# Scale and offset of the first feed-forward norm moved from GpSimd to VectorE

## The reference

```
x1  = x + attention(x, context)
h   = ln(ln(x1, g2, be2), gf, bf)          # two norms, one after the other
x2  = x1 + gelu(h @ w1 + b1) @ w2 + b2
ln(x, g, b) = (x - mean) * rsqrt(var + eps) * g + b
```

## Time and profile before

| | us |
|---|---|
| median of 3 runs | 493.59 (488.44 to 493.99) |
| the profiled execution | 494.68 |
| its span, first to last instruction | 492.4 |
| VectorE busy | 316.4 (64%) |
| GpSimd busy | 123.6 (25%) |
| granted TensorE clock, mean | 0.919 |

### The profile page before, as it was taken

How to read it: one execution, slowest core, us unless ns; L and a number is a source line. 1 busy time by engine, 2 the same in 40 slices (tenths; PEclk the granted TensorE clock), 3 DMA queues, 4 the chain that set the end, 5 groups by cost and what they waited for, 6 DMA issues and landing times.

```text
span 492.4 us, 20265 instructions
## 1 busy us (share of the span) xinstructions
PE 395.4 (80%) x8885; PEld 277.8 (56%) x8885; DVE 316.4 (64%) x909; ACT 262.9 (53%) x451; POOL 123.6 (25%) x113
## 2 busy tenths in 40 slices
PE   3667687998879978997899888988897888397765
PEld 1335554665557655765576647655676566255553
DVE  5433777769537894888578847787568666615331
ACT  2556455565355656564746554765565657154331
POOL 7001017024303070216021511134012401612000
PEclk9965999999789999999999989998999999879575
DMA  7766008324702382236422442236022012102200
GB/s 198 181 162 130 3 3 191 80 67 151 142 3 67 90 191 69 67 89 163 99 68 88 138 80 78 73 119 128 28 76 77 1 57 84 40 23 65 67 24 21
DMA packets 41958, 42.86 MB, mean 87 GB/s; under 512 B 3192, under 2 KB 34376, under 8 KB 41872
## 3 DMA queue, kind: packets, MB, share of 16 engines
q1 hardware_dynamic: 40420, 39.86, 31.3%
q0 software_dynamic: 624, 1.26, 1.0%
q10 hardware_dynamic: 828, 0.46, 0.3%
HBM read 23.65 MB, written 17.83 MB: 84 GB/s over the span
## 4 chain that ended last, share of the span: by engine, by line
PE 51%; DVE 24%; ACT 14%; issue 6%; POOL 3%; DMA 1%; ACTq 1%; DVEq 0%
PE dense L662 14%; DVE top L959 7%; PE dense L685 6%; ACT probs L500 5%; PE key L806 5%; DVE normed_f L941 4%; PE mixed L836 4%; PE side L866 3%; PE dense L657 3%; PE key L797 3%; DVE normed L941 3%; PE mixed L844 2%; PE dense L675 2%; ACT L500 2%; DVE q_part L948 2%
## 5 line engine op out<-in xcount | busy, mean ns | idle before, releaser
L500 ACT ACTIVATE probs<-key 128x1024 f32<-128x1024 f32 x96 | 98.3, 1024 | 94.8 <-PE key L806 52.5
L959 DVE TENSOR_REDUCE top<-query 128x8 f32<-128x1024 f32 (+1 forms) x96 | 116.9, 1218 | 32.0 <-PE query L764 30.7
L442 POOL TENSOR_TENSOR rstd_x<-var_eps_x,half 128x4 f32<-128x4 f32 x24 | 24.6, 1026 | 131.1 <-DVE var_eps_x L935 131.0
L806 PE MATMUL key<-top_row,spread 48*64 48x128 bf16 x1536 | 50.1, 228 | 6.2 <-ACT top_row L505 6.2
L866 PE MATMUL side<-cst,o_t 128*128 128x128 f32 x192 | 32.8, 296 | 19.0 <-ACT o_t L519 19.0
L836 PE MATMUL mixed<-probs,v 128*32 128x128 f32 x1024 | 42.7, 286 | 0.4 <-ACT probs L500 0.4
L797 PE MATMUL key<-q_stack,k_stack 48*64 48x128 f16 x1024 | 41.3, 224 | 0.0
L489 POOL TENSOR_TENSOR k_part<-k_full,k_part 128x512 f16<-128x512 f32 x8 | 9.3, 1160 | 127.2 <-ACT k_part L579 127.2
L806 PEld LDWEIGHTS key<-top_row,spread 48*64 48x64 bf16 x1536 | 34.6, 110 | 11.4 <-issue 4.5
L519 ACT COPY o_t<-mixed 128x256 f32<-128x256 f32 x96 | 35.3, 368 | 7.0 <-PE mixed L844 5.0
L662 PE MATMUL dense<-normed_ft,w 128*128 128x512 f32 x64 | 36.2, 693 | 0.7 <-ACT normed_ft L539 0.7
(11 more groups left out here) (116 smaller groups left out, 792.0 us busy)
## 6 DMA issues: line engine op xcount, KB each, us to landing
k_stack<-scratch_k SPq DMA_DIRECT2D x16, 384.0 KB, 6.5
q_stack<-scratch_q SPq DMA_DIRECT2D x64, 96.0 KB
scratch_k<-k_part SPq DMA_DIRECT2D x8, 512.0 KB, 3.0
scratch_k<-k_part SPq DMA_DIRECT2D x16, 256.0 KB, 2.6
scratch_q<-q_part SPq DMA_DIRECT2D x16, 256.0 KB, 2.2
k_stack<-scratch_k SPq DMA_DIRECT2D x16, 192.0 KB
x_in<-in_x SPq DMA_DIRECT2D x8, 256.0 KB, 6.9
scratch_q<-q_part SPq DMA_DIRECT2D x16, 128.0 KB, 1.9
```

Of the source, the lines that this page charges most:

```text
L500: nc.scalar.activation(probs[u.number % 2][:].rearrange("p h q -> p (h q)"), key[:].rearrange("p h x -> p (h x)"), ACT.Exp, scale=SCALE).t ...
L806: ins = nc.tensor.matmul(key[T * n:T * n + T, h, a * P:(a + 1) * P], spread[u.layer][rows, A2 * h + a, T * n:T * n + T], top_row[u.number ...
L959: nc.vector.tensor_reduce(maxima, query[:].rearrange("p h x -> p (h x)").rearrange("p (a k) -> p a k", a=w), AX_X, ALU.max, negate=True).t ...
```

## The change

The 4 TENSOR_SCALAR of the first norm and GpSimd's two passes are replaced by 8 SCALAR_TENSOR_TENSOR on VectorE: (x1 - mean) * g2 for the four tiles, then, after a wait on `s_gain`, (that) * rstd + be2 for the four tiles. The statistics of the result follow in the same slot 11, and the second norm is in slot 12 instead of 13. GpSimd's adding of b2 to x1 waits on `s_gain`, which now comes from VectorE after the first pass. Slot 14 keeps f_t.

```diff
--- before.py
+++ after.py
@@ -467,10 +467,7 @@
                 for c in due(10, s):
                     root(c, "x1")
                 for c in due(11, s):
-                    pool.wait_ge(s_norm["x1"], c + 1)
-                    nc.gpsimd.tensor_tensor(normed_f[:], normed_f[:], rows(row_g2), ALU.mult).then_inc(s_gain, 1)
                     pool.wait_ge(s_gain, c + 1)
-                    nc.gpsimd.tensor_tensor(normed_f[:], normed_f[:], rows(row_be2), ALU.add).then_inc(s_offset, 1)
                     nc.gpsimd.tensor_tensor(x1[c % 2][:], x1[c % 2][:], rows(row_b2), ALU.add).then_inc(s_x1_b2, 1)
                 for c in due(12, s):
                     root(c, "x1_again")
@@ -942,6 +939,22 @@
                                                   rstd[name][:, t:t + 1], ALU.subtract, ALU.mult)
                 ins.then_inc(s_norm[name], 1)
 
+            def gained_rows(c):
+
+                dve.wait_ge(s_rstd["x1"], c + 1)
+                for t in range(TILES):
+                    ins = nc.vector.scalar_tensor_tensor(
+                        out=normed_f[:, t, :], in0=x1[c % 2][:, t, :], scalar=mean_var["x1"][:, t, 0:1],
+                        in1=row_g2[:], op0=ALU.subtract, op1=ALU.mult)
+                ins.then_inc(s_gain, 1)
+                dve.wait_ge(s_gain, c + 1)
+                for t in range(TILES):
+                    ins = nc.vector.scalar_tensor_tensor(
+                        out=normed_f[:, t, :], in0=normed_f[:, t, :], scalar=rstd["x1"][:, t:t + 1], in1=row_be2[:],
+                        op0=ALU.mult, op1=ALU.add)
+                ins.then_inc(s_offset, 1)
+                dve.wait_ge(s_offset, c + 1)
+
             def low(name, part, c, dst, src, bias, high):
 
                 dve.wait_ge(s_high[part], c + 1)
@@ -1029,11 +1042,9 @@
                 for c in due(11, s):
                     if c > 0:
                         dve.wait_ge(s_done["f_t"], c)
-                    norm_rows(c, "x1", x1[c % 2], normed_f)
+                    gained_rows(c)
+                    stats("x1_again", normed_f, range(TILES))
                 for c in due(12, s):
-                    dve.wait_ge(s_offset, c + 1)
-                    stats("x1_again", normed_f, range(TILES))
-                for c in due(13, s):
                     norm_rows(c, "x1_again", normed_f, normed_f)
                 for c in job_due("w2a", s, "a"):
                     dve.wait_ge(s_x1_b2, c + 1)
```

## The result

| | before | changed |
|---|---|---|
| median | 493.79 us (4 runs) | 514.02 us (510.77 to 517.29, 4 runs) |
| profiled execution, span | 492.4 us | 510.4 us |
| VectorE busy | 316.4 us | 335.3 us |
| granted TensorE clock, mean | 0.919 | 0.895 |

The account below looks back on a forecast made before the run. The prediction took VectorE, without slack from the first norm to f_t, as the bound. Queue 7.4, stall 9.6 and clock 3.3 sum to 20.3 us; 494.7 + 20.3 - 1.1 = 514 us, range 500 to 521.

Parts of the forecast that it names:

- What bounds: From the first norm to f_t (transposes of normed_f), VectorE was claimed to bound the kernel with no slack.
- A maximum is late next, not the norm: Unit 15's maxima start 2.76 us later, delaying slot 13's scores; f_t comes 1.48 us later in chunk 2.
- The first pass: VectorE's four operations (x1 - mean) * g2 were to take 1.16 us a chunk.
- operations twice as slow: Rival: operations on two SBUF tensors take 0.13 us more each; about 512 us without stall, 523 with; chance 0.11.
- The second pass: VectorE's four operations times rstd plus be2 were to take about 2.4 us, GpSimd's b2 pass inside.
- no stall by b2: Rival: VectorE's four second-pass operations hold GpSimd off; 501 to 504 us, call it 503; chance 0.28.
- not slower: Rival: slot 13's scores can stand the late maximum, f_t comes earlier; 481 to 491 us, say 488; chance 0.08.
- VectorE's longer queue: Work put ahead of unit 15's maxima delays f_t by 1.48 us in chunks 2 to 6: 7.4 us.
- stall by b2: GpSimd's b2 pass gets in behind the second pass's first operation: 1.2 us in all eight chunks, 9.6 us.
- clock: TensorE's granted clock falls after longer waits in two of chunks 2, 3 and 6: 3.3 us, bounds 0 to 5.
- Chunks 0 and 7: One VectorE pass replacing two GpSimd passes on the latency chain was worth 0.3 us each, before the b2 stall.
- Root to root: The period of a chunk, 51.3 us before, was to become 52.8 or, with the stall, 54.0 us.

Follow-up runs that it names:

- dummy_11: Kernel before plus seven BN_STATS of a constant tile (1.4 us) on VectorE in slot 11, ahead of the first norm: 510.65 us, ratio 1.0345.
- dummy_15: Kernel before plus the same seven BN_STATS in slot 15, where VectorE is idle for 2.7 us: 494.26 us, ratio 0.9997.
- b2_later: Changed kernel, but GpSimd's adding of b2 waits until VectorE's second pass has ended: 508.77 us, ratio 1.0273 to the kernel before.
- b2_later_filled: b2_later plus 27 constant transposes on TensorE at the end of slot 12 in chunks 0 to 5: 498.49 us, ratio 1.0126.
- filled36: Changed kernel plus 36 constant transposes on TensorE at the end of slot 12 in chunks 0 to 5: 509.51 us, ratio 1.0337.
- b2_mid: Changed kernel, but GpSimd's adding of b2 is released by the first of the second pass's four operations: 512.99 us, one run.

## Why the prediction was right, and where it was off

**The mechanism is the one forecast**, step by step. *What bounds*: VectorE without slack from the first norm to f_t; shown by dummy_11 against dummy_15. *A maximum is late next, not the norm*: the scores of slot 13 wait 4.19 us, forecast 4.3, and f_t waits for nothing. *The first pass*: 1.13 us, forecast 1.16. The rival of operations twice as slow is out: operations with two float32 tensors in SBUF took 346 and 339 ns (medians) at 128 columns, the single-tensor norm 342, and both follow each other every 0.26 us. The Trainium skill (Vector Engine (DVE) Microarchitecture Reference, Points that are easy to get wrong) has half the throughput for this form; the trace does not show it, and the measurement decides. *The second pass*: 2.24 us, forecast 2.4, with GpSimd's pass inside. The rival "no stall by b2" is out by the pass of 2.24 us, which b2_later brings to 1.14. The one of "not slower" is out by the waits and the time.

**The terms**, measured as differences of ratios times 493 us:

| term | forecast | measured | from |
|---|---|---|---|
| VectorE's longer queue | 7.4 | 6.2 | b2_later_filled - before |
| stall by b2 | 9.6 | 10.4 | filled36 - b2_later_filled |
| clock | 3.3 | 5.5 | changed - filled36 |
| sum | 20.3 | 22.1 | |

From the intervals, the first is good to 1.5 us, the second to 2.3, the third to 6. So the first two are clear of noise, and by time alone the third is not: the changed kernel's interval is wide and takes in filled36's. It is shown by the trace: in chunks 2 to 5 f_t comes 1.24, 2.56, 1.96 and 1.55 us later than the 11.45 of the full clock, 7.3 us together. And that the clock costs time is clear of noise in b2_later against b2_later_filled.

In distance to f_t at the full clock it is 1.22 for the queue (forecast 1.48) and 1.13 for the stall (forecast 1.20). Half of what the first lacks is TensorE's last step, 0.87 us from the scores of slot 14 to f_t, forecast 1.00. The times in the table are less clean than these distances, since the clock differs between the kernels: at the half clock are 21 us before, 19 in b2_later_filled, 10 in filled36 and 41 in the changed kernel. So 5.5 holds the price of falls that the kernel before has too, and 10.4 compares two kernels of which the one with the stall had 8 us less at the half clock. Chunks 0 and 7 came out as forecast: f_t comes 0.2 and 0.3 us sooner in b2_later_filled, forecast 0.3, and 0.9 and 0.8 later with the stall (filled36), forecast 0.9.

**What was mis-sized is the clock.** It was counted as a small extra: two chunks of three falling anew at 1.6 us each, bounds 0 to 5. The trace shows it at the half level in each of chunks 1 to 6, in chunks 2 to 6 for 7 us and more at a time, where the one fall in rows 12 lasted 3.4. Root to root became 54.8, 56.3 and 55.6 us from chunk 2 to chunk 5, where queue and stall alone were forecast at 54.0. It also makes the terms depend on each other: taking the stall away gave 1.75% of time with the clock free to fall (the intervals overlap by a hair) and 2.1% with it held, and 1.4 us of added waiting a chunk cost 17 us in dummy_11. My expectations for b2_later and dummy_11, worked out from the same small term, missed by 3.8 and 4.7 us. That the total came out within 0.1 us by the medians is luck: by the ratio it is 22 us, with an interval of 16 to 28, and the larger clock term met a smaller queue term.

**What one detail of the argument got wrong**: GpSimd gets in not behind the first operation of the pass but in front of it, although that one is recorded as begun 0.04 us earlier. The price is the same. The Trainium skill's rule (SBUF — State Buffer, Who interferes with whom), that whoever issues first has the shared port for its whole instruction, agrees with b2_mid, where a lead of 0.16 us was enough; with a lead of 0.04 us in the changed kernel the recorded order and the rule differ, and the measurement decides. Which of the two really issued first there no trace shows.

## What to carry to other kernels

Before moving work to the engine that is idle on average, look in the timeline whether it is idle in that stretch, and which wait stands behind the place: 1.4 us a chunk there cost 17 us over eight chunks, the same 1.4 us four slots later nothing. Here a semaphore that released GpSimd and VectorE at once started a collision, both reading two tensors from SBUF; one wait later gave 1.75%, and 2.1% where the clock was held. Where TensorE waits, read its granted clock behind the wait: in dummy_11 and b2_later the waits cost more than their length.

## What was not expected of the hardware

- A wait of 1.86 us in place of 0.38 before one set of scores doubled the time at the 1.2 GHz level (dummy_11, 44 against 21 us between 110 and 430 us).
- A VectorE operation recorded as begun 0.04 us before GpSimd's 128x512 TENSOR_TENSOR stood still for it (1.46 us instead of 0.34, in the changed kernel); one begun 0.16 us before ran through in 0.34 (b2_mid).
- GpSimd's single-tensor mask pass held VectorE for only part of its 1.95 us. In chunk 7 of the kernel before (pass from 428.63 to 430.57) a small operation with two SBUF tensors was held to 0.64 us behind the pass's start, three of the norm's four operations then ran in their usual 0.33 us, and the fourth took 0.68, to 0.08 us behind the pass's end. Making the pass wait for the second norm brought that norm's longest operation from 684 to 346 ns.
